# Three norm stages of a decoder rewritten as straight blocks over eight groups

## The reference

```python
def _layernorm(x, axis=-1, eps=1e-05):
    m = jnp.mean(x, axis=axis, keepdims=True)
    v = jnp.var(x, axis=axis, keepdims=True)
    return (x - m) / jnp.sqrt(v + eps)

# part 5, context_mlp: the 77 context rows of the batch serve as both weights
g = gelu(x @ ctx[b].T, approximate=True)        # 1024 x 77
x = _layernorm(x + g @ ctx[b])

# part 6, local_transformer: only its final norm, inner being its result
x = _layernorm(x + inner)

# part 8, concat_context
part1 = x @ W[:, :256].T                        # W is 256 x 512
part2 = (sum of ctx[b] over its 77 rows) @ W[:, 256:].T / 77
x = _layernorm(x + part1 + part2 + bias)
```

## Time and profile before

| what | value |
| --- | --- |
| median of 3 runs | 10040.86 us (10026.58 to 10059.51) |
| time of the profiled execution | 10058.28 us |
| its span | 10056.5 us |
| granted TensorE clock, mean of the span | 0.883 of 2.4 GHz |
| PE busy | 8297.1 us, 83% |
| DVE busy | 5780.4 us, 57% |
| ACT busy | 4316.8 us, 43% |
| POOL busy | 2031.4 us, 20% |

### The profile page before, as it was taken

How to read it: one execution, slowest core, us unless ns; L and a number is a source line. 1 busy time by engine, 2 the same in 40 slices (tenths; PEclk the granted TensorE clock), 3 DMA queues, 4 the chain that set the end, 5 groups by cost and what they waited for, 6 DMA issues and landing times. The chain is left out here.

```text
span 10056.5 us, 125255 instructions
## 1 busy us (share of the span) xinstructions
PE 8297.1 (83%) x45414; PEld 4713.3 (47%) x45414; DVE 5780.4 (57%) x10917; ACT 4316.8 (43%) x7413; POOL 2031.4 (20%) x1790
## 2 busy tenths in 40 slices
PE   4878575794798988998999698888888689989998
PEld 1222144463233335654664354445434344458888
DVE  6777442003676755643662488776554365657776
ACT  3666331111355555632651367665222144444443
POOL 1111111103011101100110044334000011127775
PEclk8888765896899988999999799889988789989999
DMA  3222141121222110000000000000000123336665
GB/s 69 42 42 42 23 80 67 53 71 48 35 43 42 31 18 20 2 4 20 1 4 0 14 1 1 1 1 3 9 6 1 23 47 53 57 111 195 195 197 174
DMA packets 223368, 463.98 MB, mean 46 GB/s; under 512 B 50987, under 2 KB 90774, under 8 KB 220984
## 3 DMA queue, kind: packets, MB, share of 16 engines
q1 hardware_dynamic: 155175, 240.91, 11.8%
q0 software_dynamic: 67584, 215.02, 7.3%
HBM read 366.63 MB, written 75.53 MB: 44 GB/s over the span
## 5 line engine op out<-in xcount | busy, mean ns | idle before, releaser
L819 ACT ACTIVATE probs<-scores 128x1024 f32<-128x1024 f32 (+4 forms) x960 | 868.1, 937 | 888.5 <-PE scores L696 629.3
L908 DVE TENSOR_REDUCE row_max<-ring 128x1 f32<-128x512 f32 (+3 forms) x1792 | 1024.8, 625 | 250.3 <-PE ring L670 223.5
L696 PE MATMUL scores<-query_stack,key_stack 99*128 99x512 bf16 (+3 forms) x2816 | 850.0, 393 | 167.1 <-DVE levels L930 77.5
L3858 POOL DMA_INDIRECT r_got<-in_L_ffn_tables,r_index x768 | 779.5, 1015 | 457.2 <-DVE r_index L4154 203.7
L716 PE MATMUL outputs<-probs,head_values 128*32 128x512 f32 (+3 forms) x5632 | 782.3, 630 | 102.7 <-ACT probs L816 100.0
L816 ACT ACTIVATE probs<-levels,quant 128x1024 f32<-128x1024 uint8 x512 | 612.7, 1233 | 327.7 <-DVE levels L930 325.0
L930 DVE TENSOR_SCALAR levels<-scores 128x1024 uint8<-128x1024 f32 x512 | 607.5, 1219 | 178.4 <-PE scores L696 146.3
L670 PE MATMUL ring<-key_stack,query_stack 96*128 96x512 bf16 (+3 forms) x1792 | 607.2, 381 | 62.9 <-DMA key_stack<-normed_parts 40.1
L3676 DVE TENSOR_TENSOR_SCAN ssm_pre<-ssm_pre,added 128x1024 f32<-128x1024 f32 x256 | 571.0, 2270 | 33.0 <-ACT ssm_pre L3634 33.0
L696 PEld LDWEIGHTS scores<-query_stack,key_stack 99*128 99x128 bf16 x2816 | 257.5, 104 | 690.1 <-DVE levels L930 276.5
L3611 PE MATMUL state_sums<-term,constants 128*128 128x512 f32 x1024 | 494.8, 606 | 43.6 <-POOL term L3642 34.5
(11 more groups left out here) (669 smaller groups left out, 16111.6 us busy)
## 6 DMA issues: line engine op xcount, KB each, us to landing
joined_heads<-heads_out SPq DMA_DIRECT2D x512, 32.0 KB, 2.0
expert_w<-in_L_ffn_w SPq DMA_DIRECT2D x16, 1024.0 KB, 11.5
quant_parts<-parts SPq DMA_DIRECT2D x48, 256.0 KB, 5.0
query_stack<-quant_parts SPq DMA_DIRECT2D x48, 256.0 KB, 8.4
key_stack<-quant_parts SPq DMA_DIRECT2D x48, 256.0 KB, 8.3
query_stack<-cross_parts SPq DMA_DIRECT2D x48, 256.0 KB
normed_parts<-parts SPq DMA_DIRECT2D x48, 256.0 KB, 5.1
query_stack<-normed_parts SPq DMA_DIRECT2D x48, 256.0 KB, 8.6
```

What stands on the lines that cost most here:

```text
L696: last = nc.tensor.matmul(out[:, off:GROUP], keys, q_stack[0:rows, h, half * GROUP + off:(half + 1) * GROUP], start=True, stop=not edge)
L819: nc.scalar.activation(dst, s_ps[0:k_rows, 2 * (e % 2):2 * (e % 2) + 2, off:GROUP], ACT.Exp, scale=scale).then_inc(probs_ready, 1)
L908: nc.vector.reduce_max(row_max[:, i, qt, at:at + 1], src[:, 0:cols], AX.X).then_inc(ring_read, 1)
L3858: nc.gpsimd.indirect_dma_start(out=got[:, k % GOT_ROWS, :], out_offset=None, in_=io["L3_ffn_tables"], in_offset=bass.IndirectOffsetOnAxis( ...
```

## The change

The three loops go. A new function `norm_stretch` is called once in each part and builds one block over all eight groups, with no loop and no barrier within. Every engine runs its share of one list, `order`, whose step s holds: the product, mean, centring, sum and squares of group s, the hidden product and Gelu of group s + 1, and the variance, root, reciprocal and scaling of group s - 1. In the sixth part the sum is that of group s + 1 and is put right behind the scaling of group s - 1.

Buffers are two deep: z, the squares, the roots and the PSUM tiles hold groups g and g - 1, and each writer waits for the reader two groups back.

The variance is no longer narrow. PE multiplies C_MEAN (stationary) by the squares (moving, 512 columns), which gives the variance on all partitions at once; ACT takes a 128x512 root into a new tile `norm_spread` in SBUF, and DVE takes its 128x512 reciprocal in place. The spreading product is gone. GpSimd multiplies z by the reciprocal into the residual, and in the sixth part it also makes the sum of `inner` and the residual. The staging tiles and copies are gone, since in straight code the batch is a constant. The core of the diff:

```diff
+def norm_stretch(chip, hidden=None, product=None, addend=None, shift=None):
+    zero_mean = addend is None
+    order = []
+    for s in range(-1, GROUPS + 1):
+        order += [(kind, s + ahead) for kind, ahead in (("product", 0), ("mean", 0), ("centre", 0), ("var", -1), ("hide", 1), ("sum", 0 if zero_mean else 1), ("squares", 0), ("root", -1), ("gelu", 1), ("inverse", -1), ("scale", -1))
+                  if 0 <= s + ahead < GROUPS and not (zero_mean and kind in ("mean", "centre"))]
+    if not zero_mean:
+        for s in range(-1, GROUPS + 1):
+            at = [n for n, step_ in enumerate(order) if step_ == ("sum", s + 1)]
+            after = [n for n, step_ in enumerate(order) if step_ == ("scale", s - 1)]
+            if at and after:
+                order.insert(after[0], order.pop(at[0]))
...
+            fresh = summed if zero_mean else centred
...
+            def _(pe):
...
+                    elif kind == "var":
+                        if g >= 2:
+                            pe.wait_ge(root_ready, g - 1)
+                        for c in range(FC):
+                            pe.wait_ge(squared, FC * g + c + 1)
+                            last = nc.tensor.matmul(var_ps[:, g % 2, :], chip.c(C_MEAN), sq[:, g % 2, c, :], start=(c == 0), stop=(c == FC - 1))
+                        last.then_inc(var_ready, 1)
...
+            def _(act):
+                for kind, g in order:
+                    if kind == "gelu" and hidden:
+                        act.wait_ge(h_ready, g + 1)
+                        if g >= 2:
+                            act.wait_ge(y_ready, FC * (g - 1))
+                        nc.scalar.activation(h[:, g % 2, :], h_ps[0:CTX, g % 2, :], ACT.Gelu_apprx_tanh).then_inc(hidden_ready, 1)
+                    elif kind == "squares":
+                        if g >= 2:
+                            act.wait_ge(var_ready, g - 1)
+                        for c in range(FC):
+                            act.wait_ge(fresh, FC * g + c + 1)
+                            nc.scalar.activation(sq[:, g % 2, c, :], z[:, g % 2, c, :], ACT.Square).then_inc(squared, 1)
+                    elif kind == "root":
+                        act.wait_ge(var_ready, g + 1)
+                        if g >= 2:
+                            act.wait_ge(scaled, FC * (g - 1))
+                        nc.scalar.activation(rstd[:, g % 2, :], var_ps[:, g % 2, :], ACT.Sqrt, bias=chip.eps[:, 0:1]).then_inc(root_ready, 1)
...
+            def _(dve):
+                for kind, g in order:
+                    if kind == "sum" and zero_mean:
+                        if g >= 2:
+                            dve.wait_ge(scaled, FC * (g - 1))
+                        for c in range(FC):
+                            dve.wait_ge(y_ready, FC * g + c + 1)
...
+                    elif kind == "centre":
+                        dve.wait_ge(mean_ready, g + 1)
+                        for c in range(FC):
+                            tt(z[:, g % 2, c, :], z[:, g % 2, c, :], y_ps[:, g % 2, 0, :], ALU.subtract).then_inc(centred, 1)
+                    elif kind == "inverse":
+                        dve.wait_ge(root_ready, g + 1)
+                        nc.vector.reciprocal(rstd[:, g % 2, :], rstd[:, g % 2, :]).then_inc(inverse_ready, 1)
...
+            def _(pool):
+                tt = nc.gpsimd.tensor_tensor
+                for kind, g in order:
+                    if kind == "sum" and not zero_mean:
+                        if g >= 2:
+                            pool.wait_ge(scaled, FC * (g - 1))
+                        for c in range(FC):
+                            tt(z[:, g % 2, c, :], addend(g, c), x(g, c), ALU.add).then_inc(summed, 1)
+                    elif kind == "scale":
+                        pool.wait_ge(inverse_ready, g + 1)
+                        for c in range(FC):
+                            tt(x(g, c), z[:, g % 2, c, :], rstd[:, g % 2, :], ALU.mult).then_inc(scaled, 1)
...
 def context_mlp(chip):
-        with nc.Fori(0, BATCH) as b:
...
+        norm_stretch(chip, hidden=hidden)
 def concat_context(chip):
-        with nc.Fori(0, BATCH) as b:
...
+        norm_stretch(chip, product=w, shift=lambda g, c: shift[:, g // HALVES, c:c + 1])
 def local_transformer(chip):
-        with banks(nc, "norm_psum", [P, 8, GROUP], F32) as ps, nc.Fori(0, GROUPS // 2) as pair:
...
+        norm_stretch(chip, addend=lambda g, c: inner[:, c, g * GROUP:(g + 1) * GROUP])
```

More of the change, by code:

```diff
@@ L2015, in context_mlp, with hidden @@
         rows = ctx.enter_context(sbuf(nc, "context_rows", [CTX, BATCH, DIM], F32))
-        stage = ctx.enter_context(sbuf(nc, "context_stage", [P, FC, CTX], F32))
-        stage_rows = ctx.enter_context(sbuf(nc, "context_stage_rows", [CTX, 1, DIM], F32))
-        h = ctx.enter_context(sbuf(nc, "hidden", [CTX, 2, GROUP], F32))
         load(nc, [(rows[:, :, :], io["ctx"].rearrange("(b s) d -> s b d", b=BATCH))])
         centre_products(chip, [rows])
-        halves = SEQ // GROUP
-        with nc.Fori(0, BATCH) as b:
[L2023 to L2046, removed]
+        def hidden(g):
+            b = g // HALVES
+            return lambda c: chip.ctx_t[:, c, b * CTX:(b + 1) * CTX], lambda c: rows[:, b, c * P:(c + 1) * P]
+        norm_stretch(chip, hidden=hidden)
 def concat_context(chip):
@@ L2057, in concat_context @@
         shift = sb("context_shift", [P, BATCH, FC])
-        shift_b = sb("context_shift_now", [P, FC])
         load(nc, [(w[:, :, :], io["L2_xattn_w"].rearrange("(c p) n -> p c n", p=P)), (bias[:, :], io["L2_xattn_b"])])
@@ L2076, in _ @@
                     last.then_inc(shift_ready, 1)
-        with nc.Fori(0, BATCH) as b:
[L2078 to L2084, removed]
-                add_norm(chip, [tok(0), tok(1)], norm_ps, product=(w[:, 0:FC, :], lambda j, k: chip.xt[:, k, tok(j)]), bias=shift_b, zero_mean=True)
+        norm_stretch(chip, product=w, shift=lambda g, c: shift[:, g // HALVES, c:c + 1])
 def spiking_ffn(chip):
@@ L2620, in local_transformer @@
                 gated_ffn(chip, layer, weights, inner)
-        with banks(nc, "norm_psum", [P, 8, GROUP], F32) as ps, nc.Fori(0, GROUPS // 2) as pair:
-            tok = lambda g: bass.ds((pair * 2 + g) * GROUP, GROUP)
-            add_norm(chip, [tok(0), tok(1)], ps, ready=lambda g, c: inner[:, c, tok(g)])
+        norm_stretch(chip, addend=lambda g, c: inner[:, c, g * GROUP:(g + 1) * GROUP])
 class Tile:
```

47 lines of the change are left out of this document (added).

## The result

The changed kernel took 10079.1 us against 10046.2 us before (medians of 20 runs each), a ratio of 1.0033 with a 95% interval of 1.0026 to 1.0040: slower by 33 us. The forecast was 42 us more and 10083 us. The profiled execution took only 9 us more than that of before (span 10065.6 against 10056.5 us): outside the stages it was 21 us shorter, 13 of them ahead of the first stage and 10 between the first and the second. The change doesn't touch these parts, so the three stages are what to compare.

A forecast was written before the change was run, and what follows sets the result against it. No engine is full in the three stages; the written order and two-group sums buffer close a chain through all engines. Stage changes +8.3, +38.7 and -4.9 us sum to +42 us, 10083 us; range 10045 to 10110 us.

The forecast's parts named there:

- The loop: All three stages: one closed chain of scale, sum, square, root, reciprocal through the engines; six periods plus start and end.
- Rival B: All three stages: the second buffer suffices, each runs at its busiest engine; together -49 us, 9992 us; chance 8%.
- point of decision: Overlap decides once the mean of the three stages' periods is under 9.0 us.
- rival A: Matmul clock: PE stays at full speed through gaps, periods 10.0, 12.4 and 8.87 us; +25 us, 10066 us; chance 17%.
- Prices: New work in the stages: root 0.687 us on ACT, reciprocal 3.35 us on DVE, GpSimd product 1.22 us, 2.45 a pair.
- Rival C: GpSimd is dearer, at 1.8 us an operation: +74 us, 10115 us; chance 10%.
- PE's loop: First stage: product, variance, hidden product, then Gelu; 7.5 us at full matmul speed, 11.3 us at half.
- Third stage: Chain of 8.87 us a period with 0.35 us for five hand-offs; change -4.9 us.
- First stage: Chain of 10.0 us with the Sqrt load, PE's loop 11.3 us at half speed, 10.5 us taken; change +8.3 us.
- Second stage: Period 12.4 us at full speed, 15.15 at half with variance the later branch, 14.6 taken; change +38.7 us.
- Table loads: First stage: 14 loads of 1.28 us against 8 now, 7 for Sqrt, with no drain added.
- rival D: A cost the trace cannot show, such as fetching the longer straight code: 0 to 20 us; chance 5%.

The follow-up runs named there:

- the deep buffer: Changed kernel with the sums buffer three groups deep instead of two: stages 72.6, 103.1 and 56.9 us; total 10373.5 us against 10359.3 us for the kernel before.
- narrow roots: Changed kernel with root and reciprocal 128x4, spread by PE, and VectorE doing all elementwise work: 10042.6 us against 10051.8 us for the kernel before.

## Why the prediction was right

*The loop.* Right in place and in kind. In the first and third stages the sum is released by POOL in 11 of 12 periods (once by PE, with the same idle time), the reciprocal in all by ACT, and the deep buffer removed the wait for the scaling from the two stages that it could: 2.8 us a period in the third and 2.6 us in four of the six periods of the first (2.45 and a hand-off in the chain). Rival B, overlap, is refuted for this kernel, and its point of decision was set well: the three periods average 10.8 us against its 9.0.

*Which forecast was nearer.* The stages moved by 30.4 us, and that lies nearer to rival A's +25 than to the forecast's +42. A's mechanism did not hold, since half-speed records stand in all three stages; but in the first and third they lay beside other work, so that the periods were A's 10.0 and 8.87 us or less. Every stage came out below its forecast, together by 12 us. That the total of 10079 us lies only 4 us from the 10083 us forecast is in part luck: the kernel before has a median of 10046.2 us over 20 runs and not 10040.9, and the kernel moved by 33 us where its stages moved by 30.

*Prices.* The reciprocal was right to 0.01 us. GpSimd's operation was 1.26 to 1.27 us, in the predicted 1.07 to 1.285 but near its upper end; the pair, overlapped, 2.5 against 2.45 us. Rival C is refuted. Four workings of the prediction don't come out. The low end of GpSimd's price moves the total by 8 us and not 4 (56 operations in the chains at 0.15 us). The range's ends by its own terms are 10049 and 10114 us, not 10045 and 10110. The 7.5 us of PE's loop at full speed are more than the terms named (5.2 + 0.6 + 0.5 = 6.3 us): the loop that bounded the first stage at 7.4 us, once the reciprocal was narrow, runs through ACT's two table loads and not through PE's six matmuls. And the 32 and 16 matmuls of a pair are records, two to a matmul.

*Third stage.* Forecast -4.9, measured -6.7: the period was 8.65 and not 8.87 us, because the five hand-offs came to some 0.1 us and not 0.35. GpSimd begins 0.08 us after the reciprocal, the others follow 0.03 us behind, and the root's record begins 0.09 us before that of the squares ends (7043.32 against 7042.19 + 1.22).

*First stage.* Forecast +8.3, measured +5.5. The step that was mis-sized is the matmul clock: I took 10.5 us between 10.0 and 11.3. PE did alternate between its two speeds, but lay under the scaling each time, so the low end held: 9.97 us.

*Second stage.* Forecast +38.7, measured +31.6. Period 13.66 and not 14.6: the mean ran at half speed, as expected, the variance at full speed in every period (1.88 us for four records), so the variance was not the later branch. With the mean at full speed too the period was 12.30 us, where the prediction has 12.4. The first reciprocal came 1.3 us earlier than worked out.

*Table loads.* 14, as counted. The Trainium skill, "ScalarE: Activation LUTs", section "What ACT_TABLE_LOAD costs", would add 1.38 us of drain to each; the trace has 3738.90 + 1.28 and the root at 3740.20, 0.02 us later, so this case disagrees again.

*Sum.* The stages moved by 30.4 us, the kernel by 33. That nothing behind them moves was right as far as 3 us can tell, and rival D's cost is not seen; no run tested D by itself.

## What to carry to other kernels

Before an engine gets work "beside" the others, follow one buffer round: if the writer waits for the reader two groups back and every engine runs one in-order list, the period is the sum along that loop, and work moved to an idle but slower engine lengthens it. One more buffer shortens it only where no queue still holds the producer behind the consumer: here 2.8 us of 8.65 in the third stage and nothing in the second. A wide elementwise form of a per-row value (512 columns instead of 4) must be priced first where it stands in the loop: here 3.35 us for 0.18.

## What the hardware showed that was not expected

With seven unused matmuls PE idled for 2.3 us in each period of 13.65 us, and the next 3.5 us of matmuls ran at the lower level (1.2 GHz) every time, though the window's mean grant was 0.88. With nine, on another chip, it idled for 0.6 us, and they ran at 2.4 GHz but for the first record or so. In that run the first such mean, after 2.05 us of idle time, also took 2.25 us for its four records, while with narrow roots, on the same chip, one after 2.20 us took 3.75 us. So idle times this close together had different outcomes, and these rows give no length of a gap that decides. A high mean clock of a window does not say that the matmuls on the critical path had it.
